# Products of the identity in TensorE's gaps, and one set of weight products moved, in a four-layer perceiver on one core

## The reference

```python
x = x + L0_xattn(ctx, norm(x))      # one-head attention of the tokens over 257 context rows
x = x + L0_attn(norm(x))            # gated linear attention, layer norm, output product
x = x + L0_ffn(norm(x))             # 1 shared and 8 routed gated experts, top 2
x = x + L1_xattn(norm(x), ctx, mask)
x = x + L1_attn(norm(x))            # 16 heads within each sequence, causal
x = x + L1_ffn(norm(x))             # 4 experts; a gate and a small network choose how many
x = x + L2_xattn(norm(x), ctx, bias)   # attention, norm, feed-forward, norm
x = x + L2_attn(norm(x))            # attention that mixes sequences, relative positions
x = x + L2_ffn(norm(x))             # four rounds of a mixture of 4 experts
x = x + L3_xattn(norm(x), ctx)
x = x + L3_attn(norm(x))
x = x + L3_ffn(norm(x))             # low rank
```

## Time and profile before

| | us |
|---|---|
| median of three runs | 1323.85 |
| the three runs | 1321.80, 1323.85, 1324.77 |
| the profiled execution, its own time | 1324.02 |
| the profiled execution, its span | 1322.2 |

### The profile page before, as it was taken

How to read it: one execution, slowest core, us unless ns; L and a number is a source line. 1 busy time by engine, 2 the same in 40 slices (tenths; PEclk the granted TensorE clock), 3 DMA queues, 4 the chain that set the end, 5 groups by cost and what they waited for, 6 DMA issues and landing times.

```text
span 1322.2 us, 29209 instructions
## 1 busy us (share of the span) xinstructions
PE 1150.5 (87%) x10033; PEld 843.7 (64%) x10033; DVE 691.6 (52%) x2019; ACT 612.3 (46%) x1286; POOL 380.5 (29%) x551
## 2 busy tenths in 40 slices
PE   4766998999999898899997365799999999999797
PEld 1334665688777565688874154477777767888575
DVE  2276445455555543577774243634333446777653
ACT  2153223434333543577774232434343446777653
POOL 2014300121121104255550060132140504555440
PEclk8587999999999977899998657799999999999978
DMA  9510012122222001355430201011211110111000
GB/s 287 164 64 1 24 36 65 40 52 50 60 50 55 2 2 35 110 147 154 140 104 1 37 13 42 10 51 49 60 49 60 48 52 22 33 28 41 16 3 17
DMA packets 71018, 75.22 MB, mean 57 GB/s; under 512 B 6289, under 2 KB 63713, under 8 KB 70553
## 3 DMA queue, kind: packets, MB, share of 16 engines
q1 hardware_dynamic: 67880, 66.18, 18.5%
q0 software_dynamic: 1152, 6.97, 1.5%
q10 hardware_dynamic: 1904, 0.98, 0.5%
HBM read 71.49 MB, written 0.52 MB: 54 GB/s over the span
## 4 chain that ended last, share of the span: by engine, by line
PE 78%; DVE 7%; ACT 5%; DMA 4%; issue 2%; POOL 1%; ACTq 1%; SPq 1%; DVEq 0%; POOLq 0%
PE PS L498 13%; PE PS L510 13%; PE PS L1021 9%; PE PS L728 4%; PE PS L1031 4%; PE PS L692 4%; DMA CTX<-in_ctxT 2%; PE PS L501 2%; PE PS L679 2%; PE PS L735 2%; PE PS L1004 2%; PE PS L811 2%; PE PS L1051 2%; PE PS L1011 2%; ACT AR L1182 2%
## 5 line engine op out<-in xcount | busy, mean ns | idle before, releaser
L510 PEld LDWEIGHTS PS<-WB,AR 128*128 128x128 f32 x1568 | 189.5, 192 | 43.7 <-issue 40.2
L510 PE MATMUL PS<-WB,AR 128*128 128x128 f32 x1568 | 189.7, 275 | 0.0
L1182 ACT ACTIVATE AR<-PS,WB 128x512 f32<-128x512 f32 x160 | 110.0, 688 | 154.5 <-PE PS L498 148.4
L1021 PE MATMUL PS<-AR 128*128 128x257 f32 x512 | 138.5, 393 | 2.6 <-POOL AR L2494 2.6
L1753 DVE SCALAR_TENSOR_TENSOR ACC<-PS,SM,ACC 128x128 f32<-128x128 f32 x192 | 54.1, 344 | 96.0 <-PE PS L510 95.0
L1021 PEld LDWEIGHTS PS<-AR 128*128 128x128 f32 x512 | 87.1, 190 | 22.6 <-issue 8.1
L498 PE MATMUL PS<-ZT,WB 128*128 128x512 f32 x208 | 101.2, 609 | 0.0
L1628 DVE TENSOR_TENSOR AR<-PS,AR 128x512 f32<-128x512 f32 (+2 forms) x71 | 49.8, 701 | 97.3 <-ACT AR L1182 41.0
L498 PE MATMUL PS<-XNT,WB 128*128 128x512 f32 x168 | 90.5, 646 | 10.2 <-DVE AR L1628 6.0
L1182 ACT ACTIVATE AR<-PS 128x512 f32<-128x512 f32 (+2 forms) x82 | 43.5, 531 | 107.9 <-PE PS L501 75.6
L1182 ACT ACTIVATE AR<-PS,SM 128x257 f32<-128x257 f32 x136 | 64.8, 476 | 39.8 <-DVE SM L1836 30.2
(11 more groups left out here) (293 smaller groups left out, 2218.3 us busy)
## 6 DMA issues: line engine op xcount, KB each, us to landing
WB<-in_units SPq DMA_DIRECT2D x49, 385.0 KB, 3.1
CTX<-in_fside SPq DMA_DIRECT2D x32, 514.0 KB, 3.9
CTX<-in_ctxT SPq DMA_DIRECT2D x96, 130.0 KB, 2.1
CTX<-in_ctxT SPq DMA_DIRECT2D x8, 520.0 KB, 4.7
CTX<-in_ctxN SPq DMA_DIRECT2D x16, 258.0 KB
CTX<-in_ctxN SPq DMA_DIRECT2D x32, 129.0 KB, 2.3
AR<-in_ctxN SPq DMA_DIRECT2D x32, 64.5 KB, 3.0
AR<-in_l1x_w POOLq DMA_DIRECT2D x1, 2048.0 KB, 7.8
```

Of the source, the lines that this page charges most:

```text
L510: m = pe.matmul(PS[:, 4 + hh, 128 * t:128 * t + 128], f_h[hh][:, c, 128 * t:128 * t + 128], WB[:, q, 2 * UNIT + 128 * c:2 * UNIT + 128 * c ...
L1021: m = pe.matmul(PS[:, 2 + g, 0:KEYS], x_qb[q][:, P * g:P * g + P], x_k[q], start=True, stop=True)
L1182: return act.activation(o, i, fn, **k)
```

## The change

A new helper on PE, `keep_clock(k, times, cols)`, multiplies the first columns of the packed weights by the identity into bank `k`, `times` times, and nobody reads the result. It is called at 17 places of the source (19 in the run, as `self_attention` runs twice), with 54 products in all: 128 by 512, but for five of 128 by 256. The second change moves `weight_products(1)` on PE from behind the output projection of the linear attention to before the transposes of `Z`, and on ACT from behind the transposed `Z` to directly behind the first weight products. The diff follows the order of the program, PE first and ScalarE last; the piece with `c_spread(1)` is the end of `self_attention`, and the one with `gate_mm` stands in layer 1's feed-forward layer.

```diff
+            def keep_clock(k, times, cols=512):
+
+                for _ in range(times):
+                    pe.matmul(PS[:, k, 0:cols], ident, W[:, 0:cols], start=True, stop=True, skip_group_check=True)
...
             pe.transpose(PS[:, 7, 0:32], c_last, ident[0:32, 0:32]).then_inc(sig["last_turned"], 1)
+            keep_clock(2, 3, 256)
             turn(XN)
...
             project(l0_ct, w("l0x_o"))
+            keep_clock(2, 2)
...
-            pe.wait_ge(sig["l0a_qk"], seen.up("l0a_qk", 2))
+            pe.wait_ge(sig["l0a_act"], 1)
+            pe.wait_ge(sig["l0a_qk"], seen.up("l0a_qk"))
+            keep_clock(4, 3)
+            pe.wait_ge(sig["l0a_qk"], seen.up("l0a_qk"))
...
             weight_products(0)
             carry(X)
+            pe.wait_ge(sig["y_w_taken"], seen.up("y_w_taken", 4))
+            weight_products(1)
             turn(Z, "stream_ready")
...
             project(ZT, w("l0a_o"), half_taken)
             pe.wait_ge(sig["y_w_taken"], seen.up("y_w_taken", 4))
-            weight_products(1)
-            pe.wait_ge(sig["y_w_taken"], seen.up("y_w_taken", 4))
+            keep_clock(2, 2)
...
-            ff("l0f", XNT, second=True)
+            ff("l0f", XNT, lambda: keep_clock(5, 5), second=True)
+            keep_clock(2, 2)
...
                 c_spread(1)
+                keep_clock(2, 1, 256)
                 out_taken(1)
                 project_half(1, w(o))
+                keep_clock(2, 1)
...
             m.then_inc(sig["gate_mm"], 1)
+            keep_clock(4, 1)
             pe.wait_ge(sig["gate_hidden"], seen.up("gate_hidden"))
...
-            ff("l1f", XNT, second=True)
+            ff("l1f", XNT, lambda: keep_clock(5, 3), second=True)
+            keep_clock(2, 2)
...
             project(OT, w("l2x_o"))
+            keep_clock(2, 1)
             turn(Z)
             ff("l2x", ZT)
+            keep_clock(2, 9)
...
             out_taken(1)
+            keep_clock(2, 8)
             pe.wait_ge(sig["pair_out_landed"], 16 * 11)
...
             project(OT, w("l2a_w2"), hidden)
+            keep_clock(4, 6)
...
             for r in range(4):
                 moe_round(r)
+            keep_clock(2, 2)
...
             project(OT, w("l3x_o"))
+            keep_clock(2, 1)
             self_attention("l3a_q", "l3a_k", "l3a_v", "l3a_o", 5, False, 10)
...
             weight_products(0)
+            weight_products(1)
             norm(lambda t: ar(4096 + P * t, P), Z)
             turned(ZT[:, :])
-            weight_products(1)
             norm(carried_tile, XN)
```

## The result

The changed kernel takes 1307.56 us (median of 5 runs, 1305.59 to 1311.51), the kernel before, run beside it, 1321.8 us (5 runs, 1319.75 to 1324.77). The ratio is 0.9888, with a 95% interval of 0.9868 to 0.9908: 14.8 us faster [12.2 to 17.5]. The forecast was 1309.7, 14.2 us faster, so the total came out as predicted. The parts did not: two of the eight terms (B and G) brought next to nothing, two (D and E) were too small, F came at other places than told, and the reason given for the largest uncertainty, that transposes do not hold the clock, was wrong.

What follows compares the result with a forecast made beforehand. The prediction took PE, with 78% of the chain and stretches at half clock, to bound the kernel. Its terms summed to 14.2 us, taken from 1324.02 to give 1309.8 (median 1309.7), range 1299 to 1318.

Steps and rivals of the forecast that it cites:

- B: Layer 0's gate chain: five fillers let the second `up` run at full clock; gain 2.9 us [2.4 to 2.9].
- G: Gate products of layers 0 and 1, a filler ahead of both: 0.5 us each, 1.0 [-1.1 to 3.9].
- D: Boundaries behind three closed feed-forward layers, two fillers each: next sublayer starts fast; 3.6 us [-1.8 to 5.9].
- E: Layer 2 attention, eight fillers in a DMA wait of 9.97 us: faster projection behind; 0.7 us [0 to 1.2].
- F: Fillers with a norm and eight transposes behind: clock mostly still falls, only later; 2.1 us [0 to 9.2].
- A: Linear attention, weight products moved: 3.8 us wait goes, root for `Z` 1.5 later; gain 2.2 us [0.6 to 2.4].
- F's first place: Behind layer 0's cross attention, filler before a norm and eight transposes: gain 0.7 us.
- five fillers are 4.3 us and fit: Layer 0's gate chain: the fillers fit in PE's 5.99 us idle time before the second `up`.
- C: Layer 1's gate chain: three fillers start slow, speed up, and help the next `up`; 1.7 us [0.6 to 1.7].
- H: One filler in layer 1's small gate network wait, three at the very start: 0 us [-1.0 to 1.7].
- So I count real products and not transposes: Step from windows at 427.52 (clock held) and 700.59 (clock fell): transposes do not hold PE's clock.
- Rival 1: Whole kernel: whatever PE executes holds the clock, transposes too; every term at its upper end, 28.9 us, time 1295; chance 0.12.

## Why the prediction was right, and where not

The total was right: 14.2 predicted, 14.8 measured. PE had 78% of the chain, the two clock levels were in the rows, and the price of half clock was read from equal products at both levels. By term:

- **A**, moved weight products, 2.2 [0.6 to 2.4]: 1.7 over the two stages. The mechanism is as told: the 3.82 us wait went and the root for `Z` came 1.7 us later in its place (1.5 predicted). That the move needs the fillers ahead of it was the lower end; alone it is worth nothing measurable. In five other profiles with move and fillers the root was on time and the two stages gained 3.7 to 3.8 us, above the range. There no slow stretch stood at the place of 73.97, so that the products ahead (L632) took 3.17 us instead of 4.88: that part belongs to F's first place.
- **B**, layer 0's gate chain, 2.9 [2.4 to 2.9]: too large. Norm to norm the layer gained 1.4, gate products included, and three kernels without any filler there took 1.4 to 2.0 us less than the kernel before too: in this execution the five fillers brought nothing that can be told from chance. The step that failed is "five fillers are 4.3 us and fit" in an idle time of 5.99. The products ahead of the gap became faster too, while VectorE's gate chain did not, so the gap grew to nearly 8 us, 3.38 stayed open, and the clock fell once more at 132.00. With seven fillers the stage gains 3.1, and with five 3.0 to 3.4 where less of the gap was left.
- **C**, layer 1's gate chain, 1.7 [0.6 to 1.7]: 1.7. From the first `up` to the third it took 12.99 us (514.53 - 501.54) and takes 11.29 (508.55 - 497.26). One assumption was wrong without effect: the fillers did not start at half clock. Only the second `up` counts: from the first to the second it is 7.7 us in all thirteen profiles compared above, whether the first is slow or fast. In three of the seven profiles with three fillers the first `up` was fast, the idle time left longer, and the second slow again (2.93 to 3.14 us).
- **D**, closed boundaries, 3.6 [-1.8 to 5.9]: too small. From the reciprocal to the product that follows the first real ones the three places gained 0.9, 1.8 and 1.8, in sum 4.5, and the kernel with these fillers alone 6.6 [4.8 to 8.6]. (Part of that may be chance: behind the second boundary the stage gained 3.1 and 3.0, 1.2 to 1.3 more than the boundary, since a slow stretch that the kernel before had from 693.76 did not come; it was missing too in the kernel with the move alone.) I had cut the terms to six or seven tenths because transposes follow the filler; the experiment with transposes shows that there was no ground for the cut.
- **E** and **F** at layer 2, 0.7 and 0.4: 1.3 each. From the start of the projection behind the attention to the next norm's reciprocal it is 2.90 us instead of 4.19, and behind the nine fillers the twelve records of L480 take 5.40 us instead of 7.55, of which 1.3 arrive by the difference of the stages. In the other profiles the same stage gained anything from 0.2 to 5.7 us with these fillers and 0.9 to 3.9 without them, so only the local times are shown. Here too the fall of the clock "all the same" did not come.
- **F** elsewhere: nothing behind layer 0's cross attention (0.7 predicted; slow at 73.97 as before at 72.53) and nothing behind the projection of layer 2's (0.4; slow at 695.20 as before at 704.00), 0.4 instead of 0.2 behind layer 2's attention, and 1.3 instead of 0.4 in layer 3, where a slow stretch at 1291 us is gone; five other kernels with the same filler there still have one.
- **G**, gate products, 1.0: nothing arrived. In layer 1 they take 3.58 us as before. In layer 0 they are fast (1.95 us), but from the first of them to the second `up` it is 14.85 us (130.79 - 115.94), against 14.92 before (131.53 - 116.61). VectorE's gate chain starts 2.3 us earlier and then takes longer: its first two instructions are 1.41 and 1.82 us (118.31, 119.75) instead of 0.97 and 0.69 (120.61, 121.62). Why is open.
- **H**, 0: the one filler in layer 1's small gate network ran at full clock (1.12 us) and its product took 1.94 us instead of 3.57. I had given it nothing; but the kernel with the move alone has 1.94 us there too, with no filler. Against that stands the 0.9 us that the filler at the start may cost.

So the right total is in part luck: B, G and two places of F were too large, D, E and one place of F too small. Nor do the range's ends follow as told: the ends of D, F and G, added up, give 1297 to 1319 for the sum and not 1303 to 1316. Nothing in the forecast hangs on that.

The failed reasoning is in the step "So I count real products and not transposes". It rested on two windows, one of them with the busy time of isolated records. (All eight records at 700.59 are transposes; the real products start at 704.15, behind the window.) The Trainium skill (TensorE: Matmul & The Clock Gate, Part 4) says the same of transposes; in this case dense transposes kept the granted clock at 1.00 over 12 us with waits, and the whole kernel took 1305.47 us with them, so the measurement decides against it here. The Trainium skill (the same page, Part 1), which puts the ramp under 1% of a typical kernel's span, was outweighed as the prediction had argued: this kernel had 26 slow stretches and not one, the change won 1.1%, and 164 us of 1305.8 at half clock are still left. Rival 1 had the transposes right and the price wrong: 1295 took every term at its upper end, but 16 slow stretches remain.

Open is what property of PE's work holds the clock. The runs give only cases: 512-column products and dense transposes did, 32-column products without a pause did not, half-filled gaps mostly did not. Open is also where slow stretches fall in one execution: the changed kernel's profile has one from 428.96 to 432.37, at the end of layer 1's cross attention, the kernel before has none there, and nine of the twelve experiments do, though no kernel changes that code. It takes back 1.6 us of the gain.

## What to carry to other kernels

A cheap product into a free bank can be worth more than the time that it takes, where the granted clock falls behind a gap and PE is on the chain. Fill the gap nearly whole, with wide products or dense transposes, and not past its end; measure the gap again once the work ahead of it has become fast, since a gap that another engine sets grows by what PE wins. Do not judge how busy PE was from isolated records, and judge single places by the trace: over 1300 us, runs of one kernel here differ by 3 to 16 us, and the same stage of kernels with the same code there by up to 4.7 us (the stage with the long fillers).

## What the runs showed of the hardware that I had not expected

- Transposes back to back take 0.11 us each at full clock, three on their own 1.10 us by their records (722.12), and a long row of them kept the clock at full speed (1.00 over 713.58 to 725.65, until real products came).
- 32-column products without any pause were at half clock after about 3 us, for 22 and 28 us until they ended.
- A 32-column product with a 128x128 weight costs 0.22 us at full clock, not a sixteenth of the 0.86 of a 512-column one: a quarter.
- Half of the filling brought an eighth of the gain, 1.9 us [-0.3 to 4.0] of 14.8, and spread the runs over 14 us.
- Making PE faster ahead of a gap that VectorE sets moved nothing behind it: 14.85 us against 14.92 from gate products to second `up` in layer 0, 7.7 us from first to second `up` in layer 1.
